# Mamba, mixture of experts and feed-forward on one core: the decay logs in two rounded parts, spread one chunk an iteration

## The reference, cut to what matters

```
h  = rmsnorm(x);  z, xBC, dt = split(h @ in_proj.T)       # 512, 640, 8 columns
xBC = silu(causal_conv4(xBC) + b);  xs, B, C = split(xBC)
dt = softplus(dt + dt_bias);  A = -exp(A_log)             # 8 heads
state_t = state_{t-1} * exp(dt_t * A) + dt_t * x_t * B_t;  y_t = C_t . state_t + D * x_t
h  = rmsnorm(y * silu(z)) @ out_proj.T + x                # Mamba
h  = h + top-2-of-8 experts(rmsnorm(h))                   # silu between two products
x1 = layernorm(x + h)
out = layernorm(x1 + (silu(x1 @ wg * sg) * (x1 @ wu * su)) @ wd * sd)   # FF, int8 weights
```

## Time and profile before

| what | before |
|---|---|
| median of 3 runs | 1174.09 us |
| profiled execution | 1173.58 us, its span 1172.0 us |
| mean granted TensorE clock | 0.988 |
| TensorE busy | 1106.3 us, 94% |
| VectorE, ScalarE, GpSimd busy | 684.1, 618.1, 372.8 us |

### The profile page before, as it was taken

The page is one execution under the profiler, slowest core; times in us unless marked ns, Lnnn a source line. Parts: engine busy times, 40 slices in busy tenths (PEclk is TensorE's granted clock), DMA queues, the critical chain, the costliest instruction groups (busy, mean ns, idle before and its releaser), DMA issues.

```text
span 1172.0 us, 21801 instructions
## 1 busy us (share of the span) xinstructions
PE 1106.3 (94%) x7492; PEld 983.4 (84%) x7493; DVE 684.1 (58%) x1651; ACT 618.1 (53%) x1276; POOL 372.8 (32%) x331
## 2 busy tenths in 40 slices
PE   4799999999999999889999999999999999999995
PEld 3587878787878786789999999999999997888885
DVE  4686767676777776677332332323233257889875
ACT  4665655555656564254454545445454555556653
POOL 1323134334343435347404030404040225445101
PEclk9999999999999999889999999999999999999998
DMA  3030102020201011238231313313131223213101
GB/s 119 1 112 4 39 1 77 1 73 6 69 10 63 15 46 53 88 119 278 88 115 36 117 45 116 116 45 106 49 114 45 81 70 115 69 59 113 46 19 54
DMA packets 40340, 81.70 MB, mean 70 GB/s; under 512 B 5840, under 2 KB 30032, under 8 KB 38992
## 3 DMA queue, kind: packets, MB, share of 16 engines
q1 hardware_dynamic: 22768, 35.47, 9.1%
q0 software_dynamic: 7440, 35.66, 8.9%
q10 hardware_dynamic: 10064, 9.70, 2.4%
HBM read 48.05 MB, written 31.72 MB: 68 GB/s over the span
## 4 chain that ended last, share of the span: by engine, by line
PE 66%; DVE 13%; issue 9%; ACT 7%; POOL 2%; SPq 1%; DMA 1%; DVEq 0%; ACTq 0%; POOLq 0%
PE e_bank L1161 6%; PE e_bank L1178 6%; PE e_bank L1180 6%; PE e_bank L1179 6%; PE e_bank L1162 6%; PE e_bank L1163 6%; PE f_bank L1300 4%; PE f_bank L1299 4%; PE bank L1042 3%; DVE decay L1479 2%; PE bank L1068 2%; PE f_bank L1312 2%; PE f_bank L1313 2%; PE bank L957 2%; PE bank L1111 2%
## 5 line engine op out<-in xcount | busy, mean ns | idle before, releaser
L1565 DVE TENSOR_TENSOR e_h_lo<-e_bank,e_h_hi 128x512 fp32r<-128x512 f32 x148 | 102.1, 691 | 283.3 <-ACT e_bank L761 283.0
L1161 PE MATMUL e_bank<-e_x_hi,e_w_hi 128*128 128x256 f32 x592 | 169.7, 287 | 1.4 <-issue 1.3
L1178 PE MATMUL e_bank<-e_w_hi,e_h_hi 128*128 128x256 f32 x592 | 170.5, 288 | 0.5 <-DVE e_h_lo L1565 0.5
L1163 PE MATMUL e_bank<-e_x_hi,e_w_lo 128*128 128x256 f32 x592 | 168.4, 285 | 0.0
L1162 PE MATMUL e_bank<-e_x_lo,e_w_hi 128*128 128x256 f32 x592 | 168.4, 284 | 0.0
L1180 PE MATMUL e_bank<-e_w_hi,e_h_lo 128*128 128x256 f32 x592 | 167.6, 283 | 0.0
L1179 PE MATMUL e_bank<-e_w_lo,e_h_hi 128*128 128x256 f32 x592 | 167.5, 283 | 0.0
L759 ACT ACTIVATE e_h_hi<-e_bank 128x512 fp32r<-128x512 f32 x148 | 88.4, 598 | 77.1 <-PE e_bank L1163 73.0
L1429 DVE SCALAR_TENSOR_TENSOR conv<-raw,conv_w,conv 128x512 f32<-128x512 f32 x120 | 95.3, 795 | 42.2 <-ACT conv L679 39.4
L1161 PEld LDWEIGHTS e_bank<-e_x_hi,e_w_hi 128*128 128x128 f32 x592 | 114.6, 194 | 3.0 <-issue 3.0
L1162 PEld LDWEIGHTS e_bank<-e_x_lo,e_w_hi 128*128 128x128 f32 x592 | 114.6, 194 | 0.0
(11 more groups left out here) (249 smaller groups left out, 2689.4 us busy)
## 6 DMA issues: line engine op xcount, KB each, us to landing
e_stage<-in_w POOLq DMA_DIRECT2D x9, 2048.0 KB, 8.0
e_x_rows<-sent_rows SPq DMA_DIRECT2D x37, 256.0 KB
back_rows<-e_y_rows ACTq DMA_DIRECT2D x37, 256.0 KB, 2.2
x_in<-in_x SPq DMA_DIRECT2D x8, 512.0 KB, 4.4
x_res_dram<-x_res SPq DMA_DIRECT2D x8, 512.0 KB, 2.9
f_res<-x_res_dram SPq DMA_DIRECT2D x8, 512.0 KB, 3.8
out<-f_out_t SPq DMA_DIRECT2D x8, 512.0 KB, 2.6
back_rows<-zeros SPq DMA_DIRECT2D x12, 256.0 KB, 3.3
```

The source lines that it names most:

```text
L1161: mm(out, w1h[:, k, t], x_hi[:, k], start=k == 0, stop=False)
L1163: r = mm(out, w1l[:, k, t], x_hi[:, k], start=False, stop=k == KD - 1)
L1178: mm(out, eh_hi[:, k, t], w2h[:, k], start=k == 0, stop=False)
L1565: tt(flat(eh_lo[:, 2 * p:2 * p + 2]), h_ps[p][:], flat(eh_hi[:, 2 * p:2 * p + 2]).bitcast(F32), ALU.subtract).then_inc(es["h_lo_ready"], 1)
```

## The change

It has these parts.

- la is kept for two groups and also as two rounded parts, `la_parts` (high, and the rest). GpSimd spreads both into `la_t` (two instructions a chunk), and `seg` makes two products of rounded numbers with a rounded triangle `gt_r` in place of one float32 product.
- One chunk is spread in each quarter: chunk 0 of group g in w = 1, 1 in w = 2, 2 in w = 3, 3 in w = 0 of the next.
- `dt_proj` moves from w = 1 to w = 0 (around `seg` of chunk 2), `softplus_in` from w = 2 to w = 0, `softplus` on ScalarE from w = 2 to w = 0 without its own table load, `softplus_out` from w = 2 to w = 1. The convolutions and their activations take other places.
- `xm` has three buffers; the second half of a group's `send` moves from w = 2 to w = 3.
- FF start: GpSimd gathers group 1 before it takes the power for group 0; VectorE mixes group 1 before the first unit; `f_scale1(1)` and `f_transposes(1)` come two and one units sooner.
- FF end: the last group is finished in three pieces of 2, 1 and 1 chunks, each with its own DMA; the last chunk's product goes to a PSUM bank of its own.

```diff
-LA_T, DECAYS, CONVS, X_INS = 2, 6, 3, 3
+LA_T, DECAYS, CONVS, X_INS, XMS = 2, 4, 3, 3, 3
-            la_t = sb("la_t", [P, LA_T, NH, P])
+            la_t = sb("la_t", [P, LA_T, 2, NH, P], F32R)
...
             def spread(g, c, it):
-                nc.gpsimd.tensor_tensor(la_t[:, n % LA_T], bcast(la[:, c, :], 2, P), bcast(le[:], 1, NH), ALU.mult)\
-                    .then_inc(s["lat_ready"], 1)
+                for part, ready in ((0, "la_hi_ready"), (1, "la_lo_ready")):
+                    pool.wait_ge(s[ready], g + 1)
+                    nc.gpsimd.tensor_tensor(la_t[:, n % LA_T, part], bcast(la_parts[:, g % 2, part, c, :].bitcast(F32), 2, P),
+                                            bcast(le[:], 1, NH), ALU.mult).then_inc(s["lat_ready"], 1)
...
+                if ahead and w:
+                    spread(g, w - 1, it)
+                if w == 0 and 0 <= g - 1 < NG:
+                    spread(g - 1, 3, it)
...
-                if w == 2 and 0 <= g - 3:
+                if w == 3 and 0 <= g - 3 < NG - 2:
                     send(g - 3, (2, 3))
...
             def softplus(g):
-                nc.scalar.preload_act_table_set("natural_log_exp_and_others")
...
-                    mm(proj_ps[seg_bank(c, h)][:], gt[:], flat(la_t[:, q % LA_T])[:, h * GT:(h + 1) * GT], start=True, stop=True)\
-                        .then_inc(s["seg_done"], 1)
+                    for part in range(2):
+                        i = mm(proj_ps[seg_bank(c, h)][:], gt_r[:], flat(la_t[:, q % LA_T, part])[:, h * GT:(h + 1) * GT],
+                               start=part == 0, stop=part == 1)
+                    i.then_inc(s["seg_done"], 1)
...
                 if w == 0:
                     if ahead:
                         tile(g, 0)
+                        dt_proj(g, 0)
+                        dt_proj(g, 1)
                     if 0 <= g - 1 < NG:
                         seg(g - 1, 2)
+                    if ahead:
+                        dt_proj(g, 2)
+                        dt_proj(g, 3)
...
+                ts(flat(la[:, g % 2]), m, DECAY_MIN, None, ALU.max).then_inc(s["la_ready"], 1)
+                nc.vector.tensor_copy(hi, flat(la[:, g % 2])).then_inc(s["la_hi_ready"], 1)
+                tt(lo, flat(la[:, g % 2]), hi.bitcast(F32), ALU.subtract).then_inc(s["la_lo_ready"], 1)
...
                 if ahead and w == 1:
-                    convolve(g, 1)
+                    softplus_out(g)
...
+            def end_stats(j):        # also end_moments(j), end_shift(j)
+                c, end = PIECES[j]
+                dve.wait_ge(fs["down_done"], CH * (NG - 1) + end)
...
```

More of the change, by code:

```diff
@@ L67 @@
 LAST = 2
+PIECES = ((0, 2), (2, 3), (3, 4))
 SPLITS = 4
@@ L448, in _ @@
                 f_fetch(g)
-            for g in range(NG):
+            for g in range(NG - 1):
                 f_store(g)
+            for j, (c, end) in enumerate(PIECES):
+                sp.wait_ge(fs["end_out"], j + 1)
+                sp.dma_start(out[NG - 1][:, c:end], f_out[:, 1, c:end]).then_inc(fs["out_stored1"], 16)
             sp.wait_ge(fs["out_stored0"], 16 * (NG // 2))
-            sp.wait_ge(fs["out_stored1"], 16 * (NG // 2))
+            sp.wait_ge(fs["out_stored1"], 16 * (NG // 2 - 1 + len(PIECES)))
         @block.gpsimd
@@ L614, in _ @@
             f_gather(1)
+            f_deviation(0, f_norm, "var_ready", "x1_ready", "rs_ready")
+            f_deviation(1, f_norm, "var_ready", "x1_ready", "rs_ready")
             pool.wait_ge(es["y_stored"], 16 * (ended + LAST + 1))
             nc.gpsimd.tensor_tensor(f_seen[:, 2:3], half[:, 0:1], half[:, 1:2], ALU.subtract)
[L617 to L620, removed]
+            f_gather(2)
+            for g in range(NG + 1):
                 if 1 <= g and g + 1 < NG:
@@ L626, in _ @@
                     f_gather(g + 3)
+            pool.wait_ge(fs["out_ready"], NG - 1)
+            for j, (c, end) in enumerate(PIECES):
+                pool.wait_ge(fs["end_var"], j + 1)
+                nc.gpsimd.tensor_tensor(f_norm2[:, 1, c:end], f_norm2[:, 0, c:end], half[:, c:end], ALU.pow)\
+                    .then_inc(fs["end_rs"], 1)
         @block.scalar
@@ L727, in normalize @@
                 act.wait_ge(s["rs3_ready"], q + 1)
-                if c == 0:
-                    wait(act, s[f"xm_sent{g % 2}"], 16 * 2 * CH * (g // 2))
-                nc.scalar.activation(xm[:, g % 2, c, :], h1[:, q % 2], ACT.Copy, scale=tail_stat[:, q % 2, 5:6])\
+                if c == 0 and g >= XMS:
+                    act.wait_ge(s[f"xm_sent{(g - XMS) % 2}"], 16 * 2 * CH * ((g - XMS) // 2 + 1))
+                nc.scalar.activation(xm[:, g % XMS, c, :], h1[:, q % 2], ACT.Copy, scale=tail_stat[:, q % 2, 5:6])\
                     .then_inc(s["xm_ready"], 1)
@@ L823, in _ @@
                     if ahead:
+                        softplus(g)
                         raw_out(g, 1)
@@ L939, in _ @@
                     f_part(n - 1)
-                if f == (3 if g else 5) and g + 1 < NG:
+                if f == 3 and g + 1 < NG:
                     f_scale1(g + 1)
@@ L947, in _ @@
             f_scale2(NG - 2)
-            f_scale2(NG - 1)
+            act.wait_ge(fs["out_stored1"], 16 * (NG // 2 - 1))
+            for j, (c, end) in enumerate(PIECES):
+                act.wait_ge(fs["end_shift"], j + 1)
+                for n in range(c, end):
+                    i = nc.scalar.activation(f_out[:, 1, n], f_y[:, 1, n], ACT.Identity, bias=f_norm2[:, 2, n:n + 1],
+                                             scale=f_norm2[:, 1, n:n + 1])
+                i.then_inc(fs["end_out"], 1)
         @block.tensor
@@ L971, in dt_proj @@
                 if c == 0:
-                    wait(pe, s["yg_ready"], CH * g - 3)
+                    wait(pe, s["yg_ready"], CH * g - 4)
+                    wait(pe, s["pex_ready"], g)
                 t = slice(c * P, (c + 1) * P)
@@ L1305, in f_down @@
                 o = down_ps[c // 2][:, (c % 2) * D:(c % 2 + 1) * D]
+                if g == NG - 1 and c == CH - 1:
+                    o = fxt_ps[0][:, 0:D]
                 if g and f % 4 == 0:
@@ L1681, in _ @@
                 if ahead and w == 0:
+                    softplus_in(g)
                     if g % 2:
@@ L1689, in _ @@
                 if ahead and w == 2:
-                    softplus_out(g)
+                    convolve(g, 3)
                 if ahead and w == 3:
```

112 lines of the change are left out of this document (68 added, 44 removed).

## The result

The changed kernel takes 1181.35 us (median of 20 runs) beside 1173.71 for the kernel before (20 runs): ratio 1.0058, 95% interval 1.0044 to 1.0072. It is slower by 0.6%; I had forecast 1159 us, 1.25% faster. The executions of the changed kernel lie further apart than before's: 1174.3 us at a mean granted clock of 0.980, 1186.6 at 0.964. The profiled one took 1183.41 us.

What follows compares the result with a forecast made beforehand. Mamba was taken as bound by TensorE's instructions for some 450 of its 515 us. Gains of 17.2 - 4.6 - 2.5 + 1.5 + 3.3 = 14.9 us gave 1159 us, range 1152 to 1166 (8 in 10: 1146 to 1171).

Steps and rivals of the forecast that it cites:

- Term 1, seg: TensorE's seg: 0.93 us a chunk in place of 1.80, 0.87 less; 24.4 us gained in the steady part.
- Term 2, the move of dt: 24 dt products, 0.11 us each, from w = 1 to w = 0: 2.7 us gained steady, paid by the start.
- Term 4, collisions, forecast 3.0: GpSimd's added spreads delay VectorE's two-input instructions where a chunk starts a sequence; 1.0 reaches TensorE three times, 3.0 us lost.
- 3a: w = 3, behind seg of chunk 1: transposes wait 0.85 us for ScalarE's first exponential; 6.0 us lost in 7 groups.
- 3b: w = 0: softplus ahead of raw_out 1 on ScalarE makes seg of chunk 3 0.35 late; 2.4 us lost in 7 groups.
- 3d: w = 2: work leaving the iteration shrinks the 1.2 us z_act stall by about 0.5; 3.5 us gained in 7 groups.
- 3c: w = 1, shortened: VectorE's list takes 11.6 of 11.7 us; 2 us lost in all for small misses.
- Steady part, forecast 17.2 gained: Mamba's steady part: 24.4 + 2.7 - 6.0 - 2.4 - 2.0 + 3.5 - 3.0 = 17.2 us gained.
- Term 5, start: Before the first scan: spreads beside convolutions bring z_act at 43, first scan about 61.7; 4.6 us lost (1 gained to 8 lost).
- Term 6: From Mamba to experts: the later second half of the sends delays the first expert rows; 2.5 us lost (0 to 5).
- Term 7, FF: Both FF ends: 1.5 us gained at the start (0 to 2.8), 3.3 at the end (2 to 5).
- the lock: Rival: in w = 1 and w = 2 VectorE waits for whole GpSimd spreads; 24 us reach TensorE, 1183 us; chance 0.12.

Runs made afterwards that it cites:

- wide_alone: The changed kernel with its dt products 128 columns wide in place of 8 and nothing else changed; ratio to before 0.9982.
- xres_first: The changed kernel with one wait added: in w = 0 GpSimd's two spreads of chunk 3 start only after x_res; ratio to before 0.9989.
- gate_first: dt_wide with TensorE's four gate products of w = 3 put ahead of the transposes that wait for decay; 1163.9 us, ratio to before 0.9913.
- seg_twice: The changed kernel with each of seg's rounded products made twice, the second pair writing over the first; ratio to before 1.0080.
- dt_wide: xres_first with the dt products 128 columns wide; ratio to before 0.9919.

## Why the prediction was wrong

- *Term 1, seg.* From the start of seg to the next product it is now 276.72 - 275.72 = 1.00 us, 0.80 less than before; forecast 0.93 and 0.87.
- *Term 2, the move of dt.* This step failed, and the forecast's sign with it. I priced the 24 products at 0.11 us each "wherever they stand". Their time is the same, but in a block in w = 0, beside a seg of half the work, TensorE's clock fell at four of six blocks, and with wide products at none: about 9 us by the ratios of wide_alone and the changed kernel. I read the clock as a property of the stage, at its upper level, and not as something that the order of the products could change. The sum has no term for it, and no rival had it.
- *Term 4, collisions, forecast 3.0.* This one failed too: mis-placed and mis-sized. I had x_res slip into the gap between spreads, or meet one, in w = 1 and w = 2. In w = 1 it did meet one (0.94 to 1.39 us, five times); xres_first leaves these as they are, so what they cost was not measured. It met both spreads of chunk 3 in w = 0, where routing stands ahead of y_in and delays VectorE, and took up to 3.46 us, not 1.7 to 2.3. What reaches TensorE is 5.1 us by the iterations and 8 us by the ratios of both pairs of kernels.
- *Term 3, new waits.* *3a* was seen as a wait of 0.75 to 0.93 us for decay in six groups, 5.0 in all (forecast 6.0). *3b* was 0.3 to 0.5 in four groups, 1.3 (forecast 2.4). *3d*: the z wait fell from 7.2 to 3.4 us in all (forecast 3.5 gained). *3c*: w = 1 lasts 12.1 to 13.2 us behind the first group, and not 11.7; w = 0 without the x_res wait (gate_first) lasts 16.1 to 17.1, forecast 16.2. One wait had no term: TensorE waited three times for la_t, 3.8 us (before 2.4 for decay at the same products), and GpSimd's list holding TensorE was one of my own signs of being wrong.
- *Steady part, forecast 17.2 gained.* The changed kernel gained 7.1 by the profile. wide_alone gained 11.6, and between 11.6 and 17.4 with its low stretches taken out; gate_first gained 21.6. Apart from the clock and x_res the terms were about right.
- *Term 5, start.* z_act came at 43.45, as forecast (43). 4.6 lost was nearly right for the executions in which the clock comes back: 5.8 to 7.4 in xres_first, wide_alone, gate_first and seg_twice. In the profiled one it was 15.3, with the clock at 0.55 from 40 to 72 us. Here too the clock was put at nothing.
- *Term 6.* The tail lost 1.2 (forecast 2.5, where the sum by its own figures gives 512.4 and not 512.1).
- *Term 7, FF.* 4.8 forecast, nothing gained (ratio 0.9999). Its start gave 0.9 of 1.5. For its end I followed the last transfer and took it for what ends the span; the transfer came 2.2 us sooner, and the span ended 6.86 us behind GpSimd's last power, as before.

The profiled execution is 24.7 us from the forecast, and its stretches give all of it: the start 10.7, the steady part 10.1, experts and FF 5.2, less 1.3 at the change between. In the medians the forecast was 14.9 us faster and the ratio says 6.8 slower, 21.7 us apart. Of them 9 are of the narrow block, 5 of x_res (8 less the 3 forecast) and 4.8 of FF; the 3 that are left are what the start lost beyond 4.6 in the better executions (1.2 to 2.8). Each of these has an uncertainty of 2 to 3 us, so that they fit is no proof. Stronger is that with both repairs the change does gain: dt_wide and gate_first are 0.9919 and 0.9913, some 10 us faster than before. Of the rivals, the lock came nearest in time (1183) and was true in its mechanism, but its place was w = 0 and its price 5 to 8 us, not 24; that its time was so near is luck.

## What to carry to other kernels

Price a moved product by what it does to the clock and not by its time alone: many narrow products in one stretch, with little wide work around them, can cost more than a wait, and the busy share doesn't show it. Look at where the stretches of low clock begin. Here products of 8 columns followed each other no faster than products of 128, so widening them to columns that nobody reads cost no time of their own. When GpSimd gets more work, look up which instruction of VectorE with two inputs in SBUF comes next to it in every phase, also in the phases in which VectorE is late. Before shortening the end of a kernel, look up which engine's last instruction the end of the span keeps its distance to.

## What was not expected of the hardware

- 24 products of 128x8 in a row, with TensorE never waiting, were followed by a granted clock of 0.5 within 1.4 us in five of seven groups; the same with 128x128 were not in any, at the same 0.11 us each.
- x_res stood through the rest of one spread and the whole of the next (3.45 us, both together 3.74); it did not get in between them.
- A start with the same work took 62.9 us with the clock at 0.5 for 10 of the last 25 us before the first scan (xres_first), and 72.4 with it at 0.5 for 30 of the last 34 (changed).
- The span ended 6.86 us behind GpSimd's last power in all 16 traces, whether the last store was 128 KB (seen landed 4.1 us before the end of the span) or 512 KB (1.9 us before it).
